# A seventh row block of the gated layer by seven products, with the mixing between its last rounds and a ring of eleven pieces

## The chip, the cores and the metric

The kernel runs on one core of a Trainium2 chip. The metric is the device time of one execution in microseconds (us). TensorE (PE) multiplies, VectorE (DVE) and ScalarE (ACT) do the element-wise work and empty PSUM, GpSimd (POOL) does some element-wise work and issues some DMAs from its own queue, SyncE (SP) issues the rest. Every engine works its own list of instructions strictly in order; they meet only through semaphores.

## The reference

The input x has 8192 rows of 256 numbers. With `xn = layernorm(x)`:

```
feats   = rfs(xn);  weights = rfs(input_weights)        # exp(dot products - norms), 256 features
s       = feats @ weights.T                             # "the mixing"
h = silu(xn @ w1.T * s1) * (xn @ w2.T * s2)             # "the gated layer", 256 -> 1024, w1 and w2 ternary
h = gelu(h @ h1.T * s3);  h = gelu(h @ h2.T * s4)       # two square layers 1024 -> 1024, ternary
g = silu(h @ w3.T * s5)                                 # 1024 -> 256
out = x + s * g
```

Everything is float32. The ternary weights are exact in a short format, so the kernel splits each activation in a high part (fp32r) and a low part (fp16) and multiplies both by the same weights: every product below stands for two passes, "high" and "low".

## The kernel before, in words

The rows are worked in 16 halves of 512 rows; two halves (h0, h1) make a tile, so there are eight tiles, t = 0 to 7. A tile runs through four stages on TensorE, one straight after the other:

1. The gated layer. Its 1024 outputs are eight row blocks of 128 (m or p = 0 to 7), each for both halves. In tile 0 each block and half is a "step" (`gate_step`): two products over 256 inputs, in two PSUM banks, 8 matmuls of 128 x 512. In tiles 1 to 7 the first SEVEN blocks are worked by a seven-product scheme (`gate_seven`) that takes the 2 x 2 of (w1 and w2) by (both halves) at once: 7 products, high and low, so 14 matmuls for what two steps do in 16. The products of blocks 0 to 3 are in eight rounds (`ROUNDS`), those of the blocks from Q = 4 on in `MORE`, one round for each of the seven products. The remaining blocks (`EIGHT = KH - SEVEN`) are steps. `TURNS` is the hand-written order of steps and later rounds on TensorE. SEVEN is 6 before, so blocks 6 and 7 are four steps in each tile.
2. The mixing (`mix`): for each half 8 products of 128 x 256 in plain float32, 16 matmul records, in two PSUM banks.
3. The two square layers, L = 0 and 1, each by seven products w = 0 to 6 of 512 x 512 (`product`), 32 matmuls of 128 x 512 each. Their weights come piece by piece (256 KB, four pieces k = 0 to 3 for one product) into `ring`, RING = 12 pieces deep.
4. The last layer (`down`), with the seven dot products of the next tile's features between.

A block that is worked by seven products costs the others more than a step does. Four results of 128 x 512 have to be made from two banks: ScalarE copies the first of three of them out of PSUM (`gate_seven` of ScalarE, lines 1132 to 1148; for odd p VectorE copies one of them, line 1601), VectorE adds the second bank (lines 1608, 1611, 1615), ScalarE applies silu to two of them (`gate_silus`, lines 1158 and 1161), and VectorE multiplies (`gate_block`, lines 1622 and 1625). The two steps of a block (one for each half) have two silus from PSUM (line 1129) and two multiplications from PSUM (line 1593) in all.

What follows on VectorE in each tile, in this order: `low` (line 1637) makes the low part of a block pair after ScalarE's `high` (line 1188); `subtract` (line 1662) makes t1 to t4 of the square layer out of the blocks; the sums of the products (line 1670 and on). Product w = 0 takes b11 (blocks 0 to 3 of h0), w = 1 takes b21 (blocks 4 to 7 of h0), w = 2 takes t2 = b22 - t1 and w = 3 takes t1 = b12 - b11. TensorE waits at the start of a product for both of its high parts, and before its first low pass, 8 matmuls in, for both of its low parts.

The ring. Piece n may be loaded once piece n - RING has been used for the last time, which is near the end of its product, since the last block of columns needs all four pieces. SP loads the pieces that lie in HBM as sums (`feed`, line 488). In tile 0 the raw pieces (products 0, 1 and 6 of the first layer, 0 and 1 of the second) are loaded from the POOL queue instead (`feed_raw`, line 626), and the same queue makes the sums of the weight blocks: `fold_round` (lines 607 to 617) is four additions of 128 x 512 and the store of one k of them, for the two layers rounds 0 to 7. The order on POOL in tile 0 is written out:

```
            for n in range(RAW, NW * Q):        # raw pieces up to 27
                feed_raw(n)
            fold_round(6)
            for n in range(NW * Q, NW * Q + Q): # 28 to 31
                feed_raw(n)
            fold_round(7)
```

Then come the raw pieces 32 to 35 (second layer, product 1), the load of w3 and its casts (lines 742 and 747), and the rows of the next tile on their way through HBM (`rows_out`, `rows_in`, lines 634 and 643), for which VectorE waits in `turn_blocks` (line 1578). Pieces 36 to 39 are the second layer's product 2.

POOL also finishes the previous tile's output: `gate_y` (line 650) and `add_y` (line 656), each four operations of 128 x 256, for one half after the other. The second pair starts when ScalarE has done `silu_out` (line 1224) in the gated stage. The buffer that they read is later t1.

Of the kernel before, what the change touches and what calls it, by code (L numbers as in the profile page):

```python
# [10 lines left out]
NB = T // P  # L11
KD = D // P
KH = H // P
Q = KH // 2
# [16 lines left out]
RING = 12  # L31
# [29 lines left out]
SEVEN = 6  # L61
EIGHT = KH - SEVEN
FIRST_BANK, OTHER_BANK = (7, 5, 2, 3, 0, 1), (4, 6, 0, 1, 2, 3)
# [10 lines left out]
TURNS = [("step", 0), ("round", 0), ("round", 1), ("step", 1), ("round", 2), ("round", 3), ("step", 2), ("round", 4), ("step", 3),  # L74
         ("round", 5), ("round", 6)]


GATED = {(m, j): i for i, (m, j) in enumerate([(0, 0), (0, 1), (1, 0), (1, 1), (6, 0), (2, 0), (2, 1), (7, 0), (3, 0), (3, 1),
                                               (6, 1), (7, 1), (4, 0), (4, 1), (5, 0), (5, 1)])}
# [3 lines left out]
PAIRS = [(4, 6), (7, 5), (4, 6), (7, 5)]  # L83
# [29 lines left out]
def build(nc, x, win, proj, cols_in, w3s_in, wT, out):  # L113
# [4 lines left out]
    with ExitStack() as ctx:  # L118
# [120 lines left out]
        def seven_places(t, p):  # L239

            b11, b12, b21, b22, t2 = (quad[at[t][0][n]] for n in ("b11", "b12", "b21", "b22", "t2"))
            if p < Q:
                return b11[:, p, :], b12[:, p, :], b22[:, p, :], t2[:, p, :]
            return b21[:, p - Q, :], b22[:, p - Q, :], t2[:, p - 2, :], t2[:, p - Q, :]
# [80 lines left out]

        def n_step(t, n):

            return n + 1 if t == 0 else 2 * KH + 2 * EIGHT * (t - 1) + n + 1
# [5 lines left out]
        def n_third(t, p):  # L334

            return SEVEN // 2 * (t - 1) + p // 2 + 1

# [468 lines left out]
        def _(e):  # L806
# [60 lines left out]
            def gate_seven(t, turn, lows):  # L867
# [6 lines left out]
                for p, n, g, begun in [(p, n, (lows, 1 - lows)[g], g) for g in range(2) for p, n in turn]:  # L874
                    cols_p = slice(p * P, (p + 1) * P)
                    done = n_seven(t, p)
                    bank = OTHER_BANK[p] if n in (1, 3, 6) else FIRST_BANK[p]
                    if begun:
                        pass
                    elif n < 2 and p < Q:  # L880
                        first_free(t, bank)
                    elif n < 2:
                        on.wait_ge((g_c12, g_silu0)[n], n_seven(t, p - 2))
                    elif n == 2:
                        on.wait_ge(t_lo, 2 * t)
# [27 lines left out]
            def mix(t, h, banks):  # L913
# [17 lines left out]
            def bank_free(t, L, w, m):  # L931

                if w == 0 and L == 0:
                    if t == 0:
                        on.wait_ge(*((turned_f, 4) if m < 2 else ((silu, gated)[m - 2], 2 * KH - 1)))
                    else:
                        on.wait_ge((g_silu0, g_c12)[m // 2], n_seven(t, Q + m % 2))
                elif w == 0:
                    on.wait_ge(gelu["b21"], n_block(t, 0, m))
                elif w == 1 and L == 0:  # L940
                    on.wait_ge(mixed, 4 * t + m + 1)
# [108 lines left out]
            for t in range(NT):  # L1050
# [34 lines left out]
                mix(t, h0, (4, 5))  # L1085
                mix(t, h1, (6, 7))
# [29 lines left out]
        def _(e):  # L1116
# [14 lines left out]
            def gate_seven(t, turn):  # L1131

                for p, n in turn:
# [11 lines left out]
                    elif n == 4 and p % 2 == 0:  # L1145
                        if p >= Q:
# [3 lines left out]
            def gate_silus(t, part, ps_):  # L1150

                for p in ps_:
                    _, _, c21, c22 = seven_places(t, p)
                    if part == 0:
                        on.wait_ge(strassen_mm, n_turn(t, p, 5))
                        if p >= Q:
# [14 lines left out]
            def high(t, L, w, g):  # L1171
# [4 lines left out]
                elif L == 0:  # L1176
                    on.wait_ge(gated, n_gate(2 * t + int(name[2]) - 1, Q * (int(name[1]) - 1) + 2 * g + 1))
# [116 lines left out]
            for t in range(NT):  # L1294
# [20 lines left out]
                if t:  # L1315
# [20 lines left out]
                for n in range(0 if t else KH):  # L1336
# [15 lines left out]
                mixed_out(t, h0, (4, 5))  # L1352
                if t:
                    high(t, 0, 1, 0)
                mixed_out(t, h1, (6, 7))
# [99 lines left out]
        def _(e):  # L1455
# [130 lines left out]
            def gate(t, n):  # L1586
# [3 lines left out]
                on.wait_ge(silu, n_step(t, n))  # L1590
                if t == 0 and name == "b22":
# [25 lines left out]
            def gate_block(t, p):  # L1617

                c11, c12, c21, c22 = seven_places(t, p)
                on.wait_ge(g_silu0, n_seven(t, p))  # L1620
                on.wait_ge(g_c11, n_seven(t, p))
                e.scalar_tensor_tensor(out=c11, in0=c11, scalar=scale_col(1, p), in1=c21, op0=ALU.mult, op1=ALU.mult).then_inc(gated, 1)
                on.wait_ge(g_silu1, n_seven(t, p))
                on.wait_ge(g_c12, n_seven(t, p))
                e.scalar_tensor_tensor(out=c12, in0=c12, scalar=scale_col(1, p), in1=c22, op0=ALU.mult, op1=ALU.mult).then_inc(gated, 1)
# [20 lines left out]
            def subtract(t, L, i, g):  # L1646

                for name in SUMS[i][1:]:
                    if name[0] == "t":
                        on.wait_ge(block_sum, n_sum(t, L, int(name[1]) - 1, g))  # L1650
                    elif L == 0:
                        on.wait_ge(gated, n_gate(2 * t + int(name[2]) - 1, Q * (int(name[1]) - 1) + 2 * g + 1))
# [4 lines left out]
                elif L == 0 and i == 0:  # L1657
                    on.wait_ge(pool_out, NB * (n_y(2 * t - 2) + 1))
                if t == 0 and L == 0 and i == 1:
# [118 lines left out]
            for t in range(NT):  # L1778
# [33 lines left out]
                if t:  # L1812
# [199 lines left out]
```

## Time and profile before

| | us |
|---|---|
| median of 3 runs | 1257.03 (1256.8 to 1257.27) |
| the profiled execution's own time | 1258.56 |
| its span | 1256.8 |
| TensorE busy in the span | 1245.0 (99%) |
| VectorE busy | 1023.1 (81%) |
| ScalarE busy | 925.2 (74%) |
| GpSimd busy | 277.1 (22%) |

The span is the stretch from the first to the last instruction of the profiled execution; its own time is what was measured for that same execution. Busy time is the union of an engine's instructions. The mean granted TensorE clock was 0.999 of full speed (2.4 GHz).

### The profile page before, as it was taken

The page shows a single profiled execution, that of the slowest core. Times are in us where ns is not written, and L with a number is a line of the kernel's source. Part 1 is how long each engine was busy: PE and PEld are TensorE (multiplying, and loading weights), DVE is VectorE, ACT ScalarE, POOL GpSimd, SP SyncE. Part 2 cuts the span into 40 slices and gives each one's busy share as a digit, 9 for nine tenths or more (in the row PEclk, how much of TensorE's full clock was granted, in tenths as well). Part 3 has the DMA queues.
Part 4 walks back from the last instruction along what each step waited for, and adds up shares of the span by engine and source line. Part 5 has one row for each costly group of instructions (what it writes and reads, how often), then busy time and mean ns, then how long its engine had stood idle before and what let it go on. Part 6 is the DMA issues. An engine that isn't in the chain of part 4 may idle for free.

```text
span 1256.8 us, 16576 instructions
## 1 busy us (share of the span) xinstructions
PE 1245.0 (99%) x5982; PEld 821.0 (65%) x5982; DVE 1023.1 (81%) x1406; ACT 925.2 (74%) x1405; POOL 277.1 (22%) x325
## 2 busy tenths in 40 slices
PE   8999999999999999999999999999999999999997
PEld 6665676666766666666666666666676666766666
DVE  7979879877898778977889778888788877887675
ACT  4556667788677796777877778777787777787664
POOL 7964322020221102211022110311104030040000
PEclk9999999999999999999999999999999999999999
DMA  9589942575225752257413574145731466323431
GB/s 353 222 334 287 330 171 84 174 228 167 110 96 167 221 184 79 101 187 228 164 68 128 182 231 138 68 143 185 233 118 68 165 189 216 109 84 135 148 137 36
DMA packets 97351, 209.48 MB, mean 167 GB/s; under 512 B 13424, under 2 KB 16624, under 8 KB 96240
## 3 DMA queue, kind: packets, MB, share of 16 engines
q1 hardware_dynamic: 80032, 156.98, 36.7%
q0 software_dynamic: 17232, 51.39, 13.4%
q8 instruction: 49, 0.80, 0.2%
q14 instruction: 38, 0.31, 0.1%
HBM read 175.78 MB, written 38.83 MB: 171 GB/s over the span
## 4 chain that ended last, share of the span: by engine, by line
PE 96%; DVE 2%; DMA 1%; ACT 1%; issue 0%; SPq 0%
PE ps L971 62%; PE ps L899 11%; PE ps L1030 9%; PE ps L827 6%; PE ps L926 4%; DMA quad<-in_win 1%; PE ps L1006 0%; PE ps L1003 0%; PE ps L995 0%; PE ps L992 0%; PE ps L987 0%; PE ps L984 0%; PE ps L999 0%; DVE split_lo L1637 0%; DMA xin<-in_x 0%
## 5 line engine op out<-in xcount | busy, mean ns | idle before, releaser
L971 PE MATMUL ps<-split_hi,ring 128*128 128x512 f32 x1792 | 453.5, 404 | 1.4 <-ACT split_hi L1188 1.4
L971 PE MATMUL ps<-split_lo,ring 128*128 128x512 f16 x1792 | 406.3, 380 | 0.0
L971 PEld LDWEIGHTS ps<-split_hi,ring 128*128 128x128 f32 x1792 | 336.8, 188 | 83.8 <-ACT split_hi L1188 1.9
L1637 DVE SCALAR_TENSOR_TENSOR split_lo<-quad,split_hi 128x1024 f16<-128x1024 f32 x224 | 278.9, 1253 | 131.0 <-ACT split_hi L1188 130.4
L971 PEld LDWEIGHTS ps<-split_lo,ring 128*128 128x128 bf16 x1792 | 166.5, 98 | 214.2 <-issue 29.4
L1188 ACT ACTIVATE split_hi<-quad 128x1024 fp32r<-128x1024 f32 x224 | 231.6, 1048 | 33.7 <-PE ps L971 32.0
L1232 ACT ACTIVATE quad<-quad,cols_s 128x512 f32<-128x512 f32 x192 | 136.3, 719 | 51.8 <-DVE quad L1670 29.5
L1662 DVE TENSOR_TENSOR quad<-quad 128x1024 f32<-128x1024 f32 x128 | 157.2, 1261 | 0.0
L650 POOL TENSOR_TENSOR quad<-quad,s 128x256 f32<-128x256 f32 x56 | 52.0, 957 | 382.6 <-ACT quad L1224 382.6
L634 POOL DMA_DIRECT2D z_h<-xin x56 | 55.7, 1001 | 99.6 <-DVE xin L1498 99.6
L684 POOL DMA_DIRECT2D seen<-in_h x32 | 17.6, 551 | 250.0 <-ACT signs L1269 250.0
L1240 ACT ACTIVATE quad<-ps 128x512 f32<-128x512 f32 x64 | 38.3, 598 | 43.4 <-PE ps L971 43.4
L1244 ACT ACTIVATE quad<-ps 128x512 f32<-128x512 f32 x64 | 38.0, 593 | 30.4 <-PE ps L971 29.9
L926 PE MATMUL ps<-WS,quad 128*128 128x256 f32 x256 | 56.7, 379 | 0.4 <-ACT quad L1351 0.4
L926 PEld LDWEIGHTS ps<-WS,quad 128*128 128x128 f32 x256 | 48.6, 190 | 8.4 <-ACT quad L1351 1.2
L1643 DVE SCALAR_TENSOR_TENSOR split_lo<-quad,split_hi 128x1024 f16<-128x1024 f32 x34 | 40.8, 1221 | 16.3 <-ACT split_hi L1203 16.3
L1673 DVE TENSOR_TENSOR quad<-ps,quad 128x512 f32<-128x512 f32 x64 | 43.9, 686 | 12.4 <-ACT quad L1244 11.8
L827 PE MATMUL ps<-xT_hi,w 128*128 128x512 f32 x176 | 50.0, 411 | 0.8 <-ACT xT_hi L1291 0.8
L1242 ACT ACTIVATE quad<-ps 128x512 f32<-128x512 f32 x64 | 38.0, 594 | 16.1 <-PE ps L971 15.8
L1030 PE MATMUL ps<-w,split_hi 128*128 128x256 f32 x272 | 49.5, 325 | 0.0
L1246 ACT ACTIVATE quad<-ps,cols_s 128x512 f32<-128x512 f32 x64 | 42.6, 680 | 8.4 <-PE ps L971 8.4
L656 POOL TENSOR_TENSOR res<-res,quad 128x256 f32<-128x256 f32 x56 | 46.1, 856 | 1.1
(206 smaller groups left out, 1821.5 us busy)
## 6 DMA issues: line engine op xcount, KB each, us to landing
ring<-hs SPq DMA_DIRECT2D x428, 256.0 KB, 3.7
xin<-in_x SPq DMA_DIRECT2D x16, 512.0 KB, 4.1
s_h<-s SPq DMA_DIRECT2D x16, 512.0 KB, 2.6
seen<-in_h POOLq DMA_DIRECT2D x32, 256.0 KB, 3.9
res<-in_x SPq DMA_DIRECT2D x15, 512.0 KB, 5.5
out<-res SPq DMA_DIRECT2D x15, 512.0 KB, 3.1
z_h<-xin POOLq DMA_DIRECT2D x56, 128.0 KB, 4.0
xT_hi<-z_h POOLq DMA_DIRECT2D x14, 512.0 KB, 6.3
```

The source lines that it names most:

```text
L634: e.dma_start(z_h[j][:, :, :, c, :].rearrange("a i n j -> i n a j"), xin[j][32 * c:32 * c + 32, :, :].rearrange("i b (k a j) -> i (b k) a ...
L650: e.tensor_tensor(y_of(h)[:, b, :], y_of(h)[:, b, :], s[h % 2][:, b, :], ALU.mult).then_inc(pool_y, 1)
L656: e.tensor_tensor(res[:, b, :], res[:, b, :], y_of(h)[:, b, :], ALU.add).then_inc(pool_out, 1)
L827: mm = e.matmul(ps[:, bank, :], weights, moving, start=first and k == 0, stop=last and k == KD - 1, skip_group_check=h == 0 and m == 0)
L899: mm = e.matmul(ps[:, bank, :], short(weights) if g else weights, moving, start=n in (0, 1, 3) and not begun, stop=n in (1, 5, 6) and begu ...
L926: mm = e.matmul(ps[:, banks[b // 2], (b % 2) * D:(b % 2 + 1) * D], quad[at[t][0]["v"]][:, KD * j + r, b * P:(b + 1) * P], WS[:, r, :], sta ...
L971: mm = e.matmul(ps[:, 4 * (w % 2) + m, :], weights, moving, start=first and k == 0 and begins, stop=last and k == Q - 1 and not begins, sk ...
L1030: mm = e.matmul(ps[:, bank, col:col + D], part[:, k, tokens], moving[:, Q * kq + k, :], start=not last and col == 0 and k == 0 and g == 0, ...
L1188: e.activation(both(slots_hi[i], g), both(quad[at[t][L][name]], g), ACT.Identity, scale=POWER[L]).then_inc(hi, 1)
L1232: e.activation(q[:, m, :], q[:, m, :], ACT.Gelu, scale=col).then_inc(gelu[name], 1)
L1637: e.scalar_tensor_tensor(out=both(slots_lo[i], g), in0=both(quad[at[t][L][FAST[w][1]]], g), scalar=POWER[L], in1=both(slots_hi[i], g).bitc ...
L1662: e.tensor_tensor(dst, a, b, ALU.subtract).then_inc(block_sum, 1)
```

## The change

SEVEN goes from 6 to 7: in tiles 1 to 7 block 6 is worked by seven products too, and one step for each half (block 7) remains. `wsum`, the sums of the gate weights, grows from 768 to 896 columns in each of three rows, and RING goes from 12 to 11. In the new `TURNS` the mixing of h0 comes between rounds 4 and 5 of `MORE` and that of h1 after round 6, and other PSUM banks are used. ScalarE's `silu_out` moves behind its second step, and its and VectorE's orders are rewritten; VectorE does the second halves of the blocks 4 to 6 (needed for h1) after the low parts of b21. Block 6 uses two of the rows of t1's buffer for its silus, and waits for `pool_out` there. Tile 0 has the same steps, rounds and mixing as before.

```diff
-RING = 12
+RING = 11
-SEVEN = 6
+SEVEN = 7
 EIGHT = KH - SEVEN
-FIRST_BANK, OTHER_BANK = (7, 5, 2, 3, 0, 1), (4, 6, 0, 1, 2, 3)
+FIRST_BANK, OTHER_BANK = (7, 5, 2, 3, 7, 0, 1), (4, 6, 0, 1, 5, 2, 3)
-TURNS = [("step", 0), ("round", 0), ("round", 1), ("step", 1), ("round", 2), ("round", 3), ("step", 2), ("round", 4), ("step", 3),
-         ("round", 5), ("round", 6)]
+TURNS = [("step", 0), ("round", 0), ("round", 1), ("round", 2), ("step", 1), ("round", 3), ("round", 4), ("mix", 0), ("round", 5),
+         ("round", 6), ("mix", 1)]
-PAIRS = [(4, 6), (7, 5), (4, 6), (7, 5)]
+PAIRS = [(4, 6), (4, 6)]
+MIX0, MIX = ((4, 5), (6, 7)), ((4, 6), (7, 5))
@@ seven_places
             if p < Q:
                 return b11[:, p, :], b12[:, p, :], b22[:, p, :], t2[:, p, :]
+            if p == SEVEN - 1:
+                t1 = quad[at[t][0]["t1"]]
+                return b21[:, p - Q, :], b22[:, p - Q, :], t1[:, 3, :], t1[:, 2, :]
             return b21[:, p - Q, :], b22[:, p - Q, :], t2[:, p - 2, :], t2[:, p - Q, :]
@@ TensorE, gate_seven
+                    elif n < 2 and p == Q:
+                        on.wait_ge(g_silu0, n_seven(t, n))
                     elif n < 2:
-                        on.wait_ge((g_c12, g_silu0)[n], n_seven(t, p - 2))
+                        on.wait_ge((g_c12, g_silu0)[n], n_seven(t, p - 3))
@@ TensorE, mix
-                        elif b // 2 == j:
-                            on.wait_ge(silu, n_step(t, 2 + j))
+                        elif j == 0:
+                            on.wait_ge(*((silu, n_step(t, 1)), (gated, n_gate(*step_of(t, 1))))[b // 2])
                         else:
-                            on.wait_ge(gated, n_gate(*step_of(t, 3 - j)))
+                            on.wait_ge((g_silu0, g_c12)[b // 2], n_seven(t, Q))
@@ TensorE, the turns
+                    elif kind == "round":
+                        gate_seven(t, MORE[n], i % 2)
                     else:
-                        gate_seven(t, MORE[n], i % 2)
+                        mix(t, 2 * t + n, MIX[n])
@@ ScalarE
                     gate_seven(t, MORE[0])
+                    gate_silus(t, 1, (2, 3))
+                    gate_seven(t, MORE[2])
+                    gate_silu(t, 1)
                     silu_out(h0 - 2)
-                    gate_silus(t, 1, (2, 3))
-                    gate_silu(t, 1)
-                    gate_seven(t, MORE[2])
-                    gate_silu(t, 2)
                     gate_seven(t, MORE[4])
                     high(t, 0, 0, 0)
-                    gate_silu(t, 3)
-                    gate_silus(t, 0, (4, 5))
-                    gate_silus(t, 1, (4, 5))
                     high(t, 0, 0, 1)
+                    gate_silus(t, 1, (4,))
+                    gate_silus(t, 0, (4, 5, 6))
+                    gate_silus(t, 1, (5, 6))
@@ VectorE
                     gate_block(t, 1)
+                    gate(t, 0)
                     gate_seven(t, MORE[1])
-                    gate(t, 0)
                     gate_block(t, 2)
+                    gate_block(t, 3)
                     gate(t, 1)
-                    gate_block(t, 3)
                     gate_seven(t, MORE[4])
-                    gate(t, 2)
                     low(t, 0, 0, 0)
-                    gate(t, 3)
+                    low(t, 0, 0, 1)
                     gate_seven(t, MORE[6])
-                    gate_block(t, 4)
-                    gate_block(t, 5)
-                    low(t, 0, 0, 1)
+                    for p in range(Q, SEVEN):
+                        gate_block(t, p, (0,))
                     low(t, 0, 1, 0)
                     low(t, 0, 1, 1)
+                    for p in range(Q, SEVEN):
+                        gate_block(t, p, (1,))
```

## Rows read from the trace of the kernel before

**Rows 1.** The page's busy times: us, share of the span, instructions.

```profile
PE 1245.0 (99%) x5982; PEld 821.0 (65%) x5982; DVE 1023.1 (81%) x1406; ACT 925.2 (74%) x1405; POOL 277.1 (22%) x325
```

**Rows 2.** The page's chain that ended last, shares by engine.

```profile
PE 96%; DVE 2%; DMA 1%; ACT 1%; issue 0%; SPq 0%
```

**Rows 3.** Stretch, length, busy PE, PEld, DVE, ACT, POOL (instructions), clock, DMA share, GB/s.

```profile
487.01:499.63 12.62, 12.62 (x59) 7.79 (x57) 8.78 (x15) 10.23 (x17) 5.78 (x8) 1.00 0.40 159
499.63:513.15 13.52, 13.52 (x62) 8.11 (x61) 13.52 (x20) 11.53 (x20) 8.48 (x10) 1.00 0.01 4
513.15:519.87 6.72, 6.72 (x34) 5.92 (x32) 6.72 (x10) 5.12 (x8) 0.07 (x1) 1.00 0.64 226
519.87:541.29 21.42, 21.42 (x98) 13.49 (x97) 17.77 (x23) 16.08 (x25) 0.54 (x1) 1.00 0.38 136
```

**Rows 4.** PE in order of time, tile 3: start, us, line, operation, [idle before].

```profile
536.17 3.63 PE L971 MATMUL ps<-split_lo,ring 128*128 128x512 f16 x16
```

**Rows 5.** VectorE in order of time, tile 3, same columns.

```profile
502.25 0.74 DVE L1622 SCALAR_TENSOR_TENSOR quad<-quad,cols_s 128x512 f32<-128x512 f32 x1
...
508.97 1.22 DVE L1625 SCALAR_TENSOR_TENSOR quad<-quad,cols_s 128x512 f32<-128x512 f32 x1
...
514.36 1.27 DVE L1615 TENSOR_TENSOR quad<-ps,quad 128x512 f32<-128x512 f32 x2
...
521.83 1.22 DVE L1637 SCALAR_TENSOR_TENSOR split_lo<-quad,split_hi 128x1024 f16<-128x1024 f32 x1 [1.28 <-ACT split_hi L1188]
522.98 6.89 DVE L1662 TENSOR_TENSOR quad<-quad 128x1024 f32<-128x1024 f32 x6
...
532.18 1.21 DVE L1637 SCALAR_TENSOR_TENSOR split_lo<-quad,split_hi 128x1024 f16<-128x1024 f32 x1
```

**Rows 6.** ScalarE in order of time, tile 3.

```profile
503.42 1.10 ACT L1224 ACTIVATE quad<-quad 128x1024 f32<-128x1024 f32 x1
...
520.25 0.60 ACT L1214 ACTIVATE s<-ps 128x512 f32<-128x512 f32 x1 [1.06 <-PE ps L926]
...
538.36 1.05 ACT L1188 ACTIVATE split_hi<-quad 128x1024 fp32r<-128x1024 f32 x1
```

**Rows 7.** POOL in order of time, tile 3.

```profile
504.59 3.72 POOL L650 TENSOR_TENSOR quad<-quad,s 128x256 f32<-128x256 f32 x4 [11.73 <-ACT quad L1224]
508.39 3.78 POOL L656 TENSOR_TENSOR res<-res,quad 128x256 f32<-128x256 f32 x4
```

**Rows 8.** POOL in order of time, tile 0.

```profile
85.63 2.12 POOL L626 DMA_DIRECT2D ring<-in_h  x4
...
105.05 2.13 POOL L626 DMA_DIRECT2D ring<-in_h  x4
107.13 0.94 POOL L742 DMA_DIRECT2D w<-in_w  x1
```

**Rows 9.** PE in order of time, tile 0.

```profile
83.83 4.02 PE L971 MATMUL ps<-split_hi,ring 128*128 128x512 f32 x16
...
108.89 2.11 PE L971 MATMUL ps<-split_hi,ring 128*128 128x512 f32 x8 [1.44 <-ACT split_hi L1188]
...
114.12 4.03 PE L971 MATMUL ps<-split_hi,ring 128*128 128x512 f32 x16
```

**Rows 10.** Ring loads from POOL's queue, 104 to 108.5 us: issue to landing.

```profile
DMA to landing us min/median/max: 5.3/7.2/9.8
```

**Rows 11.** Ring loads from SP's queue, 115 to 118 us.

```profile
DMA to landing us min/median/max: 9.1/9.3/9.6
```

**Rows 12.** Ring load from SP's queue issued at 64.0 us.

```profile
DMA to landing us min/median/max: 8.4/8.4/8.4
```

**Rows 13.** Ring loads from SP's queue, 180 to 1250 us.

```profile
DMA to landing us min/median/max: 2.7/3.6/7.3
```

**Rows 14.** VectorE in order of time, tile 0, turning the next rows.

```profile
143.81 1.29 DVE L1578 STREAM_TRANSPOSE xin<-xT_hi 128x512 f32<-128x512 f32 x2
```

**Rows 15.** VectorE's low parts (L1637): durations in ns, min/median/max.

```profile
L1637 DVE SCALAR_TENSOR_TENSOR split_lo<-quad,split_hi x224: 1204/1224/2983, 29.9 to 1225.7; 128x1024 f16<-128x1024 f32 x112
```

More of the change, by code:

```diff
@@ L72 @@
 TURN = {pn: i for i, pn in enumerate(sum(ROUNDS + MORE, []))}
-TURNS = [("step", 0), ("round", 0), ("round", 1), ("step", 1), ("round", 2), ("round", 3), ("step", 2), ("round", 4), ("step", 3),
-         ("round", 5), ("round", 6)]
-GATED = {(m, j): i for i, (m, j) in enumerate([(0, 0), (0, 1), (1, 0), (1, 1), (6, 0), (2, 0), (2, 1), (7, 0), (3, 0), (3, 1),
-                                               (6, 1), (7, 1), (4, 0), (4, 1), (5, 0), (5, 1)])}
+TURNS = [("step", 0), ("round", 0), ("round", 1), ("round", 2), ("step", 1), ("round", 3), ("round", 4), ("mix", 0), ("round", 5),
+         ("round", 6), ("mix", 1)]
+GATED = {(m, j): i for i, (m, j) in enumerate([(0, 0), (0, 1), (1, 0), (1, 1), (7, 0), (2, 0), (2, 1), (3, 0), (3, 1), (7, 1),
+                                               (4, 0), (5, 0), (6, 0), (4, 1), (5, 1), (6, 1)])}
 PAIRS0 = [((6, 7), (4, 5), (2, 3))[n % 3] for n in range(2 * KH)]
-PAIRS = [(4, 6), (7, 5), (4, 6), (7, 5)]
+PAIRS = [(4, 6), (4, 6)]
+MIX0, MIX = ((4, 5), (6, 7)), ((4, 6), (7, 5))
 class Once:
@@ L324, in n_gate, with n_gate_both @@
             return 2 * KH * t + GATED[m, j] + 1
+        def n_gate_both(h, m):
+            return max(n_gate(h, m), n_gate(h, m + 1))
         def n_step(t, n):
@@ L334, in n_third @@
         def n_third(t, p):
-            return SEVEN // 2 * (t - 1) + p // 2 + 1
+            return (SEVEN + 1 - p % 2) // 2 * (t - 1) + p // 2 + 1
         def n_turn(t, p, n):
@@ L936, in bank_free @@
                     else:
-                        on.wait_ge((g_silu0, g_c12)[m // 2], n_seven(t, Q + m % 2))
+                        on.wait_ge((g_silu0, g_c12)[m // 2], n_seven(t, Q + 1 + m % 2))
                 elif w == 0:
@@ L940, in bank_free @@
                 elif w == 1 and L == 0:
-                    on.wait_ge(mixed, 4 * t + m + 1)
+                    on.wait_ge(mixed, 4 * t + ((0, 3, 1, 2)[m] if t else m) + 1)
                 elif w == 1:
@@ L1084, in _ @@
                     dots(h1, (6, 7))
-                mix(t, h0, (4, 5))
-                mix(t, h1, (6, 7))
+                    mix(t, h0, MIX0[0])
+                    mix(t, h1, MIX0[1])
                 for L in range(2):
@@ L1145, in gate_seven @@
                     elif n == 4 and p % 2 == 0:
-                        if p >= Q:
+                        if p == SEVEN - 1:
+                            on.wait_ge(pool_out, NB * (n_y(2 * t - 1) + 1))
+                        elif p >= Q:
                             on.wait_ge(gated, n_gate(2 * t + 1, p - Q))
@@ L1155, in gate_silus @@
                         on.wait_ge(strassen_mm, n_turn(t, p, 5))
-                        if p >= Q:
+                        if p == SEVEN - 1:
+                            on.wait_ge(pool_out, NB * (n_y(2 * t - 1) + 1))
+                        elif p >= Q:
                             on.wait_ge(gated, n_gate(2 * t + 1, p - 2))
@@ L1176, in high @@
                 elif L == 0:
-                    on.wait_ge(gated, n_gate(2 * t + int(name[2]) - 1, Q * (int(name[1]) - 1) + 2 * g + 1))
+                    on.wait_ge(gated, n_gate_both(2 * t + int(name[2]) - 1, Q * (int(name[1]) - 1) + 2 * g))
                 else:
@@ L1351, in _ @@
                         e.activation(quad[at[0][0]["v"]][:, n, :], stage[n % 2][:, :], ACT.Exp).then_inc(feat, 1)
-                mixed_out(t, h0, (4, 5))
+                mixed_out(t, h0, (MIX if t else MIX0)[0])
                 if t:
                     high(t, 0, 1, 0)
-                mixed_out(t, h1, (6, 7))
+                mixed_out(t, h1, (MIX if t else MIX0)[1])
                 if t:
@@ L1590, in gate @@
                 on.wait_ge(silu, n_step(t, n))
+                if t and name == "b22":
+                    on.wait_ge(gated, n_gate(2 * t, m - Q))
                 if t == 0 and name == "b22":
@@ L1615, in gate_seven, with gate_block @@
                         e.tensor_tensor(c12, B, c12, ALU.add).then_inc(g_c12, 1)
-            def gate_block(t, p):
+            def gate_block(t, p, halves=(0, 1)):
                 c11, c12, c21, c22 = seven_places(t, p)
[L1620 to L1625, printed above, removed]
+                if 0 in halves:
+                    on.wait_ge(g_silu0, n_seven(t, p))
+                    on.wait_ge(g_c11, n_seven(t, p))
+                    e.scalar_tensor_tensor(out=c11, in0=c11, scalar=scale_col(1, p), in1=c21, op0=ALU.mult, op1=ALU.mult).then_inc(gated, 1)
+                if 1 in halves:
+                    on.wait_ge(g_silu1, n_seven(t, p))
+                    on.wait_ge(g_c12, n_seven(t, p))
+                    e.scalar_tensor_tensor(out=c12, in0=c12, scalar=scale_col(1, p), in1=c22, op0=ALU.mult, op1=ALU.mult).then_inc(gated, 1)
             def rows_sums_low(t):
@@ L1651, in subtract @@
                     elif L == 0:
-                        on.wait_ge(gated, n_gate(2 * t + int(name[2]) - 1, Q * (int(name[1]) - 1) + 2 * g + 1))
+                        on.wait_ge(gated, n_gate_both(2 * t + int(name[2]) - 1, Q * (int(name[1]) - 1) + 2 * g))
                     else:
@@ L1658, in subtract @@
                     on.wait_ge(pool_out, NB * (n_y(2 * t - 2) + 1))
+                    on.wait_ge(gated, n_gate(2 * t + 1, SEVEN - 1))
                 if t == 0 and L == 0 and i == 1:
```

## The prediction
> **What bounds the kernel now.** I read the page's busy times first: TensorE 99% of the span, VectorE 81%, ScalarE 74% [rows 1]. The chain of waits agrees: 96% of it is TensorE [rows 2]. So time can be saved only by fewer matmuls, and is lost whenever TensorE waits for something that it does not wait for now. The second reading is by stretch, in tile 3, whose pattern all tiles 1 to 7 repeat [rows 3]: the eight rounds of blocks 0 to 3 (487.01 to 499.63), the turns (to 513.15), the mixing (to 519.87), three products (to 541.29). TensorE is busy in all of it, but in the turns VectorE is busy 13.52 of 13.52 us and ScalarE 11.53. VectorE enters the square layers with a debt that it pays off by the third product: there it still has 17.77 of 21.42. That debt decides what the change is worth in a tile.
>
> **What is removed from TensorE.** In each of seven tiles two steps of 8 matmuls go and 14 matmuls of one more block come: 2 fewer, and 9 changes between high and low in the turns instead of 11. The rounds have 56 matmuls in 12.62 us, the turns 28 + 32 = 60 in 13.52 us [rows 3]: 0.225 us each in both, so 2 are 0.45 us. From below: at the mixing's rate, 6.72/32 = 0.21 us, a matmul costs that much bare, the turns' other 0.92 us would be their 11 changes at 0.08, and two matmuls with two changes are 0.59 us. I take 0.5 us a tile, 3.5 us in all (3.2 to 4.1). The mixing's 32 records stay and only move.
>
> **What is added in tiles 1 to 7.** ScalarE gets 5 operations for block 6 (three copies, two silus) and loses 2 silus; VectorE gets 5 and loses 2. On VectorE that is 3 x 0.6 to 0.66 us, about 1.9 us a tile, in a stretch where it has no gap. What was cover is also cut: before, all 6.72 us of mixing lay between the last round and product 0; after, only one half's 3.36 us. Against that, 4 multiplications of the gate blocks were slowed by POOL: such a one takes 0.74 us, and 1.22 us beside POOL's output work [rows 5, 7]; after the change `silu_out` stands behind the second step, which ends 34 matmuls into the turns (499.63 + 34 x 0.225 = 507.3), and its silu of 0.6 us: 507.9 instead of 503.42 [rows 6], and POOL starts 4.5 us later, when all but the last of these blocks are done.
>
> I lay out VectorE's new order in tile 3's clock, with durations less some 0.08 us where instructions follow each other (6 subtractions in 6.89 us are 1.15 each; adds 0.60, gate blocks 0.66, low parts 1.14) [rows 5]. Round 6 now ends at 519.87 - 0.5 - 3.36 = 516.0. The three sums of round 6 run from about 515.8 to 517.6 (before, two, from 514.36 [rows 5]), the three first-half blocks to 519.6. `low` of b21's first pair follows its high part, to 521.2. The second waits: ScalarE takes it after the two evictions of h1's mixing, of which the last waits for TensorE, as it did before (520.25 [rows 6]); its high part ends at 522.0, the low part at 523.1, against 523.05 before. Then come three second-half blocks (2.0), six subtractions (6.9), two statistics (0.66), low part of t2, a sum (0.60), second low part of t2: 535.6. Before, that one ended at 532.18 + 1.21 = 533.4 [rows 5], so VectorE is 2.2 us later. TensorE's first low pass of product 2 came at 536.17 [rows 4] and now would at 535.65. The cover of 2.8 us is gone: wait 0 to 0.2. Product 3 is next: its high parts stand on ScalarE behind gelus that wait for VectorE's sums, so they move about 2 us with them, from 538.36 + 1.05 = 539.4 [rows 6] to 541.3 or 541.4; product 3 began at 541.29 [rows 3] and now would at 540.8. Wait 0.5 us. From product 4 on VectorE has caught up. The POOL window now covers the low parts of b11; such a part takes 1.2 us free and up to 2.98 beside POOL [rows 15]. There is 1.3 us of idle before round 6's sums to hide it, so I add nothing, 0.4 us at the most. So a tile waits 0.5 us more (bounds 0 and 1.2), seven 3.5 us (0 to 8.4). The gain of the fewer matmuls and this wait cancel.
>
> The Trainium skill (SBUF, Who interferes with whom) says that a VectorE instruction with two SBUF inputs contends with a GpSimd one that reads SBUF, and that one of them blocks for the whole of the other. By it each of the two low parts could stand behind a whole POOL operation, an estimate of 0.93 us each from POOL's own rows, 0.6 us more than the idle hides in a tile. The row of 1.22 instead of 0.74 us shows less than a whole operation; the sum above goes by the rows.
>
> **What the ring of eleven does.** In tiles 1 to 7 the last piece of product w + 2 is now ordered at the end of product w instead of a product earlier. A product is 21.42/3 = 7.14 us [rows 3], so it has 7.14 + 0.6 + 0.6 us to land. These loads take 3.6 us, at most 7.3 [rows 13]: hidden, nothing.
>
> Tile 0 is another matter, though it has no seven-product block. Three places:
>
> First, piece 11. It was loaded with the first twelve; now it waits for product 0's end, 64.0 us. A load issued just then took 8.4 us [rows 12], so it lands at 72.4. Product 2 starts at 57.10 + 2 x 7.14 = 71.4 (products follow from 83.83, in whose sixteen matmuls product 3 ends at 85.66 [rows 9]) and wants it at 72.0. Cost 0.4 us (0 to 1).
>
> Second, POOL's queue. `feed_raw(27)` stands before `fold_round(6)`. It waited for piece 15, used up at the end of product 3, and was the fourth of the loads from 85.63, at 87.2 [rows 8]. With eleven it waits for piece 16, used up at the end of product 4: 92.3. Everything behind it on POOL moves by 5.1 us: round 6, raw pieces 28 to 31, round 7, raw pieces 32 to 35, the load of w3, the next rows. Pieces 28 to 31 go out from 100.9 to 102.5 and are wanted from 108.9 to 109.5 [rows 9]; with the landings of rows 10 up to their median they are at most 0.2 us late. Pieces 32 to 35 went out from 105.05 and now would from 110.2 to 111.8; they landed in 5.3 to 9.8 us [rows 8, 10]. The second layer's product 1 starts at 108.89 + 7.14 = 116.0 [rows 9] and wants its fourth piece 0.65 us in. At the shortest landing, piece 35 is there at 117.1, wait 0.4; at the longest at 121.6, wait 4.9. As SP's loads of that time also take 9.1 to 9.6 us [rows 11], I take 3.5 us. A second way leads to the same size: the rows of tile 1 pass the same queue, VectorE takes them up at 143.81 without waiting [rows 14], and 5.1 us later they would hold it up in front of sums for which TensorE waits.
>
> Third, piece 39, ordered at the end of the second layer's product 0 and behind the store of round 7; it takes 9.3 us [rows 11], to 125 or, with the store late, 128 us. Product 2 would want it at 123.8, or 127.3 after the wait above. 0.4 us more (0 to 1.2).
>
> The wider `wsum` makes four POOL additions in tile 0 a sixth longer, some 1.4 us together, before the DMA store and the ring for which POOL waits anyway: nothing. Tile 0's sum is 0.4 + 3.5 + 0.4 = 4.3 us (0.4 to 7.1).
>
> **The sum.** 4.3 - 3.5 + 3.5 = +4.3 us, and 0.2 us for what of POOL's window is not hidden. The profiled execution took 1258.56 us, 1.76 over its span; the median is 1257.03, 1.5 us under it. A difference of 4.5 us does not depend on which one I start from: 1263.1 for the profiled one, 1261.5 us for the median.
>
> **The rivals.**
> *TensorE's count decides, and all else stays hidden.* For it: 99% busy, and idle of 1.28 us before one low part [rows 5] that can be filled. Against it: piece 35 late even at the shortest landing. 1257.0 - 3.5 + 0.4 = about 1253.8. Chance 0.12.
> *The steady tiles gain in full, tile 0 pays.* If VectorE's 2.2 us are 1.5, the waits of products 2 and 3 vanish: 1257.0 - 3.5 + 4.3 = 1257.8. Chance 0.20.
> *VectorE's debt is larger in every tile.* At product 3's start TensorE waits for t1's high part. It decides once the debt is over 2 us; each us more costs 7. With 1 us more than I count (the low parts beside POOL, a late piece of round 6): 1261.5 + 7 = 1268.5. Chance 0.15.
> *A long wait in tile 0 costs twice.* If the granted clock falls to its lower level (half of 2.4 GHz) after the 3.5 us, the matmuls behind it take twice as long; half a product so worked adds 3.6 us: 1265. The one wait of 1.44 us [rows 9] left the clock at 1.00, and no row here is at the lower level. Chance 0.08.
> The Trainium skill (TensorE: Matmul & The Clock Gate, Why this matters for your kernels) advises against idle gaps of TensorE between its bursts of matmuls, since the clock falls after them; that is this last rival, and no row here shows it.
>
> **How the numbers follow.** The forecast has 0.45, the rivals 0.12, 0.20, 0.15 and 0.08. A measurement of this kernel can tell 0.2%, 2.5 us, from no change. Faster than 1254.5: the first rival and a little of the second, 0.15. Within: most of the second, and the forecast's lower edge, 0.23. Slower: 0.62. Range: 1254.5, where a tile waits nothing and tile 0 pays 1 us, to 1267, where tiles wait 0.9 us and tile 0 pays 6.5. The forecast's own is 1259.5 to 1264.
>
> **What would show it.** Right: TensorE idle in tile 0 at product 1 of the second layer, released by DMA; POOL's round 6 starting near 92.8; turns plus mixing 0.5 us shorter in each tile; TensorE idle of a few tenths before products 2 or 3, released by ScalarE's split or VectorE's. Wrong: no idle in tile 0 beyond the 1.44 us, or products 2 and 3 following without a gap.

## The result and the profile after

The changed kernel takes 1263.43 us (median of 5 runs, 1262.64 to 1265.88) against 1257.09 us; the ratio is 1.005, with a 95% interval of 1.0039 to 1.0062. It is 6.3 us slower; the forecast was 4.5 us slower. The profiled execution is the slowest of the five: 1265.88 us, with a span of 1264.1 us. Its busy times, from the page's first part:

```profile
PE 1247.3 (99%) x5968; PEld 820.4 (65%) x5968; DVE 1034.6 (82%) x1427; ACT 932.4 (74%) x1426; POOL 278.7 (22%) x325
```

Against [rows 1] TensorE has 14 matmuls fewer (5968 for 5982), as counted, and is busy 2.3 us more. The profiled spans differ by 7.3 us. By stretches, from the starts of the products, of the tiles' rounds and of the last layer's last stretch (1238.84 us before, 1245.81 after):

| Stretch, us | before | after | difference |
|---|---|---|---|
| start to product 0 of tile 0 | 57.10 | 57.78 | +0.7 |
| from there to tile 1's rounds | 122.81 | 128.66 | +5.85 |
| tiles 1 to 6, each | 153.67 | 153.81 | +0.15, six times +0.9 |
| tile 7, to its last layer | 136.92 | 136.49 | -0.4 |
| the rest of the last layer | 17.92 | 18.27 | +0.35 |

The first line is chance: in the eight experiments below, with either kernel's code up to there, product 0 starts between 55.3 and 56.9 us, so both profiles here start it late. Nearly all of the loss is in tile 0, where the diff changes only the ring and the width of `wsum`.

**Tiles 1 to 7.** The stretches that answer to [rows 3], in tile 3, which starts 6.80 us later (columns as there). The mixing of h0 now lies in the second of them and that of h1 in the third, so the two are to be taken together:

```profile
493.81:506.41 12.60, 12.60 (x59) 7.79 (x57) 8.76 (x15) 10.22 (x17) 5.76 (x8) 1.00 0.44 158
506.41:519.80 13.39, 13.39 (x61) 8.93 (x60) 12.81 (x21) 12.06 (x21) 3.87 (x6) 1.00 0.00 0
519.80:526.22 6.42, 6.42 (x31) 4.89 (x31) 5.96 (x8) 4.68 (x9) 4.77 (x5) 1.00 0.29 87
526.22:547.90 21.68, 21.63 (x98) 13.47 (x96) 18.88 (x23) 15.44 (x24) 0.54 (x1) 1.00 0.54 181
```

From the first round to product 0 are 32.41 us instead of 32.86: 0.45 us gained. In the three products (the last line) VectorE is busy 18.88 us instead of 17.77: that is the debt, work that it has still to do when the square layers begin. Its instructions in order of time (start, us, line, operation, [idle before]):

```profile
519.19 3.04 DVE L1657 SCALAR_TENSOR_TENSOR split_lo<-quad,split_hi 128x1024 f16<-128x1024 f32 x2
...
522.69 1.89 DVE L1633 TENSOR_TENSOR quad<-ps,quad 128x512 f32<-128x512 f32 x3 [0.47 <-PE ps L910]
...
532.27 6.90 DVE L1683 TENSOR_TENSOR quad<-quad 128x1024 f32<-128x1024 f32 x6
...
541.47 1.21 DVE L1657 SCALAR_TENSOR_TENSOR split_lo<-quad,split_hi 128x1024 f16<-128x1024 f32 x1
```

ScalarE's high part of t1, for which product 3 waits:

```profile
547.22 1.05 ACT L1205 ACTIVATE split_hi<-quad 128x1024 fp32r<-128x1024 f32 x1
```

And the waits of TensorE's weight loads from 526 to 549 us (who, for whom: us in all, times, longest):

```profile
PEld ps L982 <- DVE split_lo L1657: 0.7, 2, 0.5
PEld ps L982 <- ACT split_hi L1205: 0.5, 1, 0.5
```

Put back by these 6.80 us, the second low part of t2 ends at 542.68 - 6.80 = 535.9 us (forecast 535.6; it was 533.4), and t1's high part at 548.27 - 6.80 = 541.5 (forecast 541.3 to 541.4). The waits are those of the side that loads weights; the matmuls themselves start some 0.2 us late in product 2 and 0.4 us late in product 3. So a tile gains 0.45 us and loses 0.6. The two low parts of b11 beside POOL took 3.04 us instead of some 2.4, mostly out of VectorE's idle time, of which 0.47 us were left.

**Tile 0.** POOL in order of time:

```profile
86.53 1.59 POOL L635 DMA_DIRECT2D ring<-in_h  x3 [0.84 <-PE ps L982]
93.44 0.54 POOL L635 DMA_DIRECT2D ring<-in_h  x1 [5.32 <-PE ps L982]
93.99 1.32 POOL L616 TENSOR_TENSOR early<-early 128x512 f32<-128x512 f32 x1
...
109.56 2.14 POOL L635 DMA_DIRECT2D ring<-in_h  x4
```

Of the four loads that stood together in [rows 8], the fourth, piece 27, now waits 5.32 us for a matmul, and the additions of round 6 behind it start at 93.99. Pieces 32 to 35 go out from 109.56 instead of 105.05: the additions took less time than before, so that of 6.2 us at round 6 (93.99 for 87.75) 4.5 are left, and 3.8 reckoned from product 0. The chain of waits has the last of them (start, us, engine, operation):

```profile
111.12 11.88 DMA ring<-in_h
```

and TensorE in the second layer's products 0 and 1 answers to [rows 9]:

```profile
111.81 2.85 PE L982 MATMUL ps<-split_hi,ring 128*128 128x512 f32 x8 [3.69 <-ACT split_hi L1205]
114.46 4.57 PE L982 MATMUL ps<-split_lo,ring 128*128 128x512 f16 x16
118.67 2.21 PE L982 MATMUL ps<-split_hi,ring 128*128 128x512 f32 x8
121.25 0.70 PE L982 MATMUL ps<-split_hi,ring 128*128 128x512 f32 x2 [0.36 <-DMA ring<-in_h]
123.04 1.66 PE L982 MATMUL ps<-split_hi,ring 128*128 128x512 f32 x6 [1.09 <-DMA ring<-in_h]
```

Piece 35 was ordered at 111.12 and landed at 123.0 us. Without a wait TensorE would have taken it up where before did, 116.0 + 0.65 + 0.7 (the later start) = 117.3 us. That is 5.7 us, nearly the whole loss of tile 0. Two things stand in front of it and cost nothing more. One is a wait of 3.69 us for the high part of the second layer's first product, where [rows 9] has 1.44. The other is the clock behind that wait, the third number from the end of these rows (stretches of 1 us, columns as in [rows 3]):

```profile
113.00:114.00 1.00, 1.00 (x4) 0.73 (x3) 1.00 (x2) 1.00 (x2) 0.00 (x0) 0.50 1.23 358
...
115.00:116.00 1.00, 1.00 (x4) 0.36 (x3) 1.00 (x2) 0.00 (x0) 0.00 (x0) 0.50 0.96 317
116.00:117.00 1.00, 1.00 (x5) 0.43 (x4) 0.41 (x1) 0.58 (x2) 0.00 (x0) 0.82 1.09 317
```

It was granted at 0.50, the lower of the two levels (1.2 of 2.4 GHz), for some 3.4 us. TensorE came later to the piece that was not there yet, and waited less for it.

### The profile page after: what moved, and what is told of

It is laid out like the page before. It is cut to its first block, busy times and chain, and to the rows that moved or that the text cites. A ratio compares the mean times of both kernels' runs of the same rounds, so it can differ in the third digit from the quotient of the medians.

```text
span 1264.1 us, 16605 instructions
## 1 busy us (share of the span) xinstructions
PE 1247.3 (99%) x5968; PEld 820.4 (65%) x5968; DVE 1034.6 (82%) x1427; ACT 932.4 (74%) x1426; POOL 278.7 (22%) x325
## 4 chain that ended last, share of the span: by engine, by line
PE 92%; ACT 2%; DMA 2%; DVE 2%; POOL 1%; issue 1%; SPq 0%
PE ps L982 58%; PE ps L910 12%; PE ps L1041 9%; PE ps L937 4%; PE ps L836 4%; DMA ring<-in_h 1%; ACT quad L1249 1%; DMA quad<-in_win 1%; DVE quad L1691 1%; DVE split_lo L1657 1%; PE ps L1014 0%; PE ps L998 0%; ACT split_hi L1205 0%; PE ps L1003 0%; PE ps L1017 0%
## 5 line engine op out<-in xcount | busy, mean ns | idle before, releaser
L659 POOL TENSOR_TENSOR quad<-quad,s 128x256 f32<-128x256 f32 x56 | 45.5, 842 | 416.6 <-ACT quad L1241 416.6
L1257 ACT ACTIVATE quad<-ps 128x512 f32<-128x512 f32 x64 | 38.3, 598 | 39.7 <-PE ps L982 39.7
L1261 ACT ACTIVATE quad<-ps 128x512 f32<-128x512 f32 x64 | 38.0, 594 | 30.5 <-PE ps L982 29.9
L665 POOL TENSOR_TENSOR res<-res,quad 128x256 f32<-128x256 f32 x56 | 53.1, 979 | 1.1
L1694 DVE TENSOR_TENSOR quad<-ps,quad 128x512 f32<-128x512 f32 x64 | 43.8, 685 | 7.6 <-ACT quad L1261 7.0
L1041 PEld LDWEIGHTS ps<-w,split_hi 128*128 128x128 f32 x272 | 36.8, 190 | 13.8 <-issue 13.7
L1691 DVE TENSOR_TENSOR quad<-ps,quad 128x512 f32<-128x512 f32 x64 | 42.4, 681 | 2.8 <-PE ps L982 2.8
## 6 DMA issues: line engine op xcount, KB each, us to landing
z_h<-xin POOLq DMA_DIRECT2D x56, 128.0 KB, 4.1
```

The source lines that it names most:

```text
L665: e.tensor_tensor(res[:, b, :], res[:, b, :], y_of(h)[:, b, :], ALU.add).then_inc(pool_out, 1)
L1041: mm = e.matmul(ps[:, bank, col:col + D], part[:, k, tokens], moving[:, Q * kq + k, :], start=not last and col == 0 and k == 0 and g == 0, ...
L1691: e.tensor_tensor(quad[v][:, m, :], here, quad[v][:, m, :], ALU.add).then_inc(c_sum["b11"], 1)
```

## The experiments

The kernel before ran beside all of them: median 1257.63 us beside the first four (27 runs, 1256.57 to 1259.5), 1257.52 us beside the last four (18 runs, 1256.61 to 1258.69). The changed kernel was not run again beside them; before stood 0.4 to 0.5 us higher there than in the first comparison, and differences to the changed kernel are uncertain by about as much. Tile 0 is from product 0 to tile 1's rounds, the period is that of tiles 1 to 6, both from the one profiled execution of each. That execution lies 2.4 us above the median for the changed kernel and for "mixes last", 1.5 to 1.6 above it for before and "both of these", and within 0.4 us of it for the other experiments.

| Kernel | median us | ratio (95%) | tile 0 | period |
|---|---|---|---|---|
| before | 1257.09 | | 122.8 | 153.67 |
| changed | 1263.43 | 1.005 (1.0039 to 1.0062) | 128.7 | 153.81 |
| ring of eleven alone | 1262.96 | 1.0045 (1.0031 to 1.0059) | 128.0 | 153.66 |
| changed, POOL's order | 1259.06 | 1.001 (1.0001 to 1.0019) | 125.0 | 153.79 |
| changed, t3 later | 1259.78 | 1.0019 (1.001 to 1.0028) | 128.4 | 153.20 |
| changed, both of these | 1256.18 | 0.9992 (0.9983 to 1.0001) | 125.3 | 153.19 |
| changed, statistics later | 1266.54 | 1.008 (1.0066 to 1.0093) | 130.5 | 153.81 |
| changed, mixes last | 1265.27 | 1.006 (1.0046 to 1.0074) | 130.5 | 154.05 |
| before, t3 later | 1257.37 | 1.0 (0.9991 to 1.0009) | 122.8 | 153.67 |
| all that helps together | 1254.08 | 0.9974 (0.9963 to 0.9984) | 123.3 | 153.20 |

### The ring of eleven alone

```
-RING = 12        (in the kernel before)
+RING = 11
```

> The kernel before with a ring of eleven pieces and nothing else. Theory (tile 0 pays for the ring, the seventh block pays and costs about nothing in tiles 1 to 7): POOL's fold round 6 moves from 87.8 to about 93, the second layer's pieces 32 to 35 land near 121 to 123, TensorE waits in tile 0 for 4 to 6 us more; time 1257.1 + 5 = 1261 to 1263; tiles 1 to 7 as before, period 153.66 us. Rival (the ring is hidden, the loss comes from the seventh block): 1257 to 1258.

One constant costs 5.3 of the 6.3 us (1262.96 - 1257.63). Tile 0 is 5.2 us longer and the period the same to 0.01 us. TensorE, same columns as above:

```profile
109.58 3.26 PE L971 MATMUL ps<-split_hi,ring 128*128 128x512 f32 x8 [3.69 <-ACT split_hi L1188]
...
120.14 1.66 PE L971 MATMUL ps<-split_hi,ring 128*128 128x512 f32 x6 [0.82 <-DMA ring<-in_h]
```

The same two waits stand in the same places, for a high part and for a piece. At least 5.2 us of tile 0's loss are the ring's, and in tiles 1 to 6 the ring costs nothing.

### The late loads taken out of the way of POOL's additions

In the changed kernel piece 27 is ordered ahead of all of fold round 6, and piece 31 ahead of round 7, so the round stands behind the piece's wait. Here each is taken out of its loop and ordered inside the round, ahead of the fourth addition (`load_round` was never called there, `beside` was None):

```
-                    load_round(beside)
+                    feed_raw(beside)
...
-            for n in range(RAW, NW * Q):
+            for n in range(RAW, NW * Q - 1):
...
-            fold_round(6)
-            for n in range(NW * Q, NW * Q + Q):
+            fold_round(6, NW * Q - 1)
+            for n in range(NW * Q, NW * Q + Q - 1):
...
-            fold_round(7)
+            fold_round(7, NW * Q + Q - 1)
```

> The changed kernel with POOL's order in tile 0 rewritten: piece 27 is loaded inside fold round 6 and piece 31 inside fold round 7 (ahead of the fourth addition), so that neither round stands behind its wait. Theory: POOL is only 1 to 2 us later than in the kernel before, pieces 32 to 35 land by 118, tile 0 loses 0 to 2 us instead of 5 to 6; time 1257.1 + 0.2 x 6 - 0.4 + 1 = 1258 to 1259.5. Rival (fewer pieces ahead are late by themselves, or the DMA queues are full): 1262 to 1264.

It took 4.4 us less than the changed kernel, tile 0 is 3.7 us shorter, and the period is unchanged. So most of the cost is not that there are fewer pieces as such, but that the wait for one holds up the rest of the queue. POOL in order of time:

```profile
84.27 1.60 POOL L635 DMA_DIRECT2D ring<-in_h  x3 [1.55 <-PE ps L982]
85.85 1.32 POOL L616 TENSOR_TENSOR early<-early 128x512 f32<-128x512 f32 x1
...
104.27 2.19 POOL L635 DMA_DIRECT2D ring<-in_h  x4
```

The additions follow the third load at once, and pieces 32 to 35 go out at 104.27. TensorE no longer waits for a DMA in front of product 1. What is left of the loss, 2.2 us, is 0.6 us more of the wait for the high part (2.07 us for 1.44) and a lower clock behind it, from 108.4 to 111.9 us, which costs half of that time (TensorE, and the stretch from 109 to 112 us):

```profile
107.92 3.38 PE L982 MATMUL ps<-split_hi,ring 128*128 128x512 f32 x8 [2.07 <-ACT split_hi L1205]
...
109.00:112.00 3.00, 3.00 (x9) 1.70 (x8) 3.00 (x4) 1.55 (x3) 0.00 (x0) 0.53 1.04 294
```

### t3's sum moved a product later

```
-                                elif w == 0:
-                                    subtract(t, 0, 2, m - 2)
+                                elif w == 0 and t == 0:
+                                    subtract(t, 0, 2, m - 2)
+                                elif t and w == 1 and m >= 2:
+                                    subtract(t, 0, 2, m - 2)
```

> The changed kernel with the two subtractions for t3 on VectorE moved in tiles 1 to 7 from product 0 to product 1, behind the low parts of t2. Theory (VectorE's debt makes TensorE wait 0.2 us in product 2 and 0.4 us before product 3): both waits go, 0.6 us a tile in six tiles, 3.6 us; time 1263.4 - 3.6 = 1259.8. Rival (the wait before product 3 hangs on ScalarE's own order): 1263.

The period fell from 153.81 to 153.20 us: 0.61 us a tile, the two waits above. It took 3.65 us less than the changed kernel. Against before the period is 0.47 us shorter, so that is what the seventh block is worth in a tile once nothing waits. Tile 0 has the same code as in the changed kernel; this profile, near the median, shows 128.4 us for it where that of the changed kernel's slowest execution shows 128.7.

### Both

> Both of the last two edits on the changed kernel. Theory: they are in different tiles and add up; 1257.1 + 1 - 0.44 x 7 = about 1255, under both kernels. Rival: the waits only move, 1258 to 1260.

The two single gains are 4.4 + 3.7 = 8.1 us. Together they are 7.3, and the time lies 1.2 us over the forecast. The kernel is 1.4 us under before in its medians, but the interval just reaches 1. Tile 0 is still 2.5 us too long:

```profile
109.26 2.14 PE L982 MATMUL ps<-split_hi,ring 128*128 128x512 f32 x8 [2.06 <-ACT split_hi L1205]
...
118.39 1.66 PE L982 MATMUL ps<-split_hi,ring 128*128 128x512 f32 x6 [1.20 <-DMA ring<-in_h]
```

The wait for the high part is as long as with POOL's order alone (2.06 for 2.07 us), but the clock stayed at 1.00 here: the 8 matmuls behind it took 2.14 us and not 3.38. Instead TensorE meets a wait of 1.20 us for the last piece, which took 11.1 us to land and not 9.6.

### The row statistics of tile 0 later

Why does that high part come late? VectorE and POOL of the changed kernel at that time:

```profile
102.45 2.12 DVE L1540 SCALAR_TENSOR_TENSOR sm<-sm 128x8 f32<-128x8 f32 x1
...
104.81 1.12 DVE L1544 SCALAR_TENSOR_TENSOR sm<-sm 128x8 f32<-128x8 f32 x1
...
106.45 0.85 DVE L1540 SCALAR_TENSOR_TENSOR sm<-sm 128x8 f32<-128x8 f32 x1
...
107.54 1.14 DVE L1544 SCALAR_TENSOR_TENSOR sm<-sm 128x8 f32<-128x8 f32 x1
...
103.23 1.31 POOL L616 TENSOR_TENSOR early<-early 128x512 f32<-128x512 f32 x1
104.62 1.28 POOL L618 TENSOR_TENSOR early<-early 128x512 f32<-128x512 f32 x1
```

The same in the kernel before:

```profile
100.82 0.66 DVE L1524 SCALAR_TENSOR_TENSOR sm<-sm 128x8 f32<-128x8 f32 x1
...
101.72 1.13 DVE L1528 SCALAR_TENSOR_TENSOR sm<-sm 128x8 f32<-128x8 f32 x1
...
103.08 1.12 DVE L1526 TENSOR_TENSOR sm<-sm 128x8 f32<-128x8 f32 x1
```

These are VectorE instructions on 8 numbers a partition; the median of their lines is 0.17 us. Four took 0.85 to 2.12 us here, 4.5 us too much in all; before, three took 0.66 to 1.13, 2.4 us too much. The difference, 2.1 us, is nearly what the wait for the high part grew by (1.44 to 3.69). The first two shown end at 104.57 and 105.93 us, POOL's two additions at 104.54 and 105.90. The Trainium skill (SBUF, Who interferes with whom) says that a VectorE instruction with two SBUF inputs and a GpSimd one that reads SBUF exclude each other for a whole instruction. The trace agrees with these two ends; but the one of 2.12 us began 0.8 us before POOL's addition, while POOL still ordered DMAs. The statistics stand in front of the sum from which the late high part is made. So they were moved behind it:

```
-... (0, 5, 2): (6, 7), (0, 5, 3): (8, 9),
-             (1, 0, 2): (10,), (1, 0, 3): (11,), (1, 1, 2): (12,), (1, 1, 3): (13,)}
+... (1, 0, 2): (6, 7), (1, 0, 3): (8, 9),
+             (1, 1, 2): (10, 11), (1, 1, 3): (12, 13)}
```

> The changed kernel with six of the small statistics operations of tile 0 moved on VectorE from the first layer's product 5 to the second layer's products 0 and 1. Theory (tile 0's end is set by pieces 32 to 35 landing near 121 to 123; the wait of 3.7 us before the second layer and the lower clock after it lie in front of that and cost nothing of their own): that wait shrinks to under 1 us, the wait for the DMA grows to 4 or 5 us, time 1262 to 1263.5, as the changed kernel. Rival (the waits add up): 3 to 4 us less, 1259.5.

It took 3.1 us more than the changed kernel, 1.8 of them in tile 0 by the profiles, and both theories missed. The wait in front of product 0 shrank to 0.35 us, now for a piece, but three of POOL's four additions of round 7 took 2.15 us each now, and pieces 32 to 35 went out from 110.80, with product 0 starting 1.3 us earlier. TensorE, and the clock behind its wait:

```profile
112.39 2.20 PE L982 MATMUL ps<-split_hi,ring 128*128 128x512 f32 x8
...
119.87 4.19 PE L982 MATMUL ps<-split_hi,ring 128*128 128x512 f32 x8 [5.28 <-DMA ring<-in_h]
...
119.80:126.00 6.20, 6.07 (x13) 3.11 (x14) 0.17 (x1) 0.00 (x0) 0.00 (x0) 0.50 1.31 377
```

The wait of 5.28 us for the DMA is nearly all that is left of waiting. The 6.2 us behind it at clock 0.50 do the work of some 3 us, and nothing is waited for after them: this lower level costs in full. It outweighs that the last piece, though ordered 2.5 us later reckoned from product 0, landed 0.6 us earlier (it took 8.7 us and not 11.9). The Trainium skill (TensorE: Matmul & The Clock Gate, Why this matters for your kernels) advises against idle gaps of TensorE between bursts of matmuls because the clock falls after them; these rows agree.

### The mixes after the last round

`TURNS` ends on `("round", 4), ("round", 5), ("round", 6), ("mix", 0), ("mix", 1)`; all else is the changed kernel's.

> The changed kernel with both halves' mixing after round 6, as in the kernel before. Theory (the low part of b21's second pair waits for the evictions of the mixing wherever it stands, so VectorE's debt is the same): waits of 0.6 us a tile stay, period 153.8, time as the changed kernel, within 1 us. Rival (the cover of 3.36 us more lets VectorE start the last sums earlier): 0.6 us a tile less, 1259.8.

It took 1.8 us more than the changed kernel, and the period is 0.24 us longer, which is 1.4 us in six tiles. Both theories missed. The waits in the square layers went, but now rounds 5 and 6 follow round 4 at once and wait for their banks (TensorE's waits from 494 to 548 us):

```profile
PEld ps L910 <- ACT quad L1163: 0.7, 1, 0.7
...
PEld ps L910 <- DVE quad L1629: 0.4, 1, 0.4
...
PE ps L910 <- ACT quad L1163: 0.3, 1, 0.3
```

From a tile's first round to its product 0 it is 33.2 us instead of 32.4. So the mixing between the rounds was cover for the work that empties their banks. Tile 0, where nothing was changed, took 130.5 us in this profile, that of the slowest execution. There the clock was at 0.50 a second time, from 121.8 to 125.2 us, behind waits of 0.62 and 1.10 us for pieces, as it was not in the changed kernel's profile behind 0.36 and 1.09; half of these 3.4 us is nearly all by which tile 0 is longer than in the changed kernel.

### t3's sum moved in the kernel before

> The kernel before with t3's subtractions moved as in e3. Theory (before, no wait of TensorE hangs on VectorE in tiles 1 to 7): no change, 1257 to 1257.6, period 153.66. Rival (VectorE's order hides some loss there too): 2 us less.

No change: ratio 1.0, period 153.67 us in both. The order of the sums is worth something only with the debt that the seventh block brings.

### All that helps, together

The edits of the fourth and the fifth experiment, and fold round 7 orders pieces 31 to 34 inside it, where the fourth has piece 31 alone; only piece 35 stays behind the round:

```
-                if beside is not None:
-                    load_round(beside)
+                for n in beside or ():
+                    feed_raw(n)
...
+            fold_round(6, (NW * Q - 1,))
...
+            fold_round(7, range(NW * Q + Q - 1, NW * Q + 2 * Q - 1))
...
-                    for n in range(NW * Q + Q, 2 * NW * Q):
+                    for n in range(NW * Q + 2 * Q - 1, 2 * NW * Q):
```

> The changed kernel with both edits of e4, the statistics moved as in e5, and pieces 31 to 34 all loaded inside fold round 7. Theory: pieces 32 to 34 go out 3 us earlier, only piece 35 is left behind, tile 0 loses under 1 us against the kernel before; time 1254 to 1255. Rival (the DMA queues are full then, so that the pieces land no earlier, or piece 39 becomes late): 1256.

1254.08 us (8 runs, 1253.51 to 1255.48): 3.4 us faster than before and 9.3 faster than the changed kernel. Tile 0 is 0.5 us longer than before's, the period 0.47 shorter. POOL and TensorE:

```profile
101.29 2.17 POOL L635 DMA_DIRECT2D ring<-in_h  x4 [0.30 <-POOL early L620]
...
105.65 0.54 POOL L635 DMA_DIRECT2D ring<-in_h  x1
...
115.19 1.64 PE L982 MATMUL ps<-split_hi,ring 128*128 128x512 f32 x6 [1.94 <-DMA ring<-in_h]
```

Reckoned from product 0 of tile 0, which started 2.5 us earlier here, the first of the late loads, piece 32, goes out 5.2 us earlier than in the changed kernel, and the last, piece 35, 3.0; a wait of 1.94 us for that last one is left, behind which the clock stayed at 1.00. A seventh block with a ring of twelve was not tried. The wider `wsum` takes 384 more numbers a partition, and a piece of the ring has 512.

## Why the prediction came out right, step by step

- **Fewer matmuls, 0.5 us a tile.** Measured 0.45 us in the stage, 0.47 us in the period once the waits are gone (the third experiment).
- **VectorE's debt, waits of 0.5 us a tile in seven.** Measured 0.6 us in six, in the places forecast and with times right to 0.3 us; moving work of VectorE behind them took them away, so that they were its debt is shown. Tile 7 has no statistics in its square layers, showed no such wait and gained 0.4 us. The sum over tiles 1 to 7 is +0.5 us, for a forecast of 0 and 0.2 us for POOL's window.
- **POOL's queue, 3.5 us.** The mechanism was right: the wait for piece 27 (5.32 us) holds up the queue, and the first experiment gives that to the ring alone. The shift forecast for all behind it, 5.1 us, was too large for the late loads: reckoned from product 0 they went out 3.8 us later. The mis-sized term is the landing of piece 35, and it outweighs that. It was taken within 5.3 to 9.8 us [rows 10], and was 11.88. The cost was 5.7 us in the profile and 5.2 in the first experiment, above the 4.9 set as its upper end. Why it landed so late is not shown; a copy of 1 MB from SP's queue was ordered half a us ahead of these loads. The second way to this size, through the rows of tile 1, cost nothing of its own: VectorE takes them up without waiting, at 150.34 us, as far behind product 1 as before.
- **Pieces 11 and 39, 0.4 us each.** Neither is waited for. Piece 11 went out at 64.7 and landed in 6.8 us, before 72.7.
- **The ring in tiles 1 to 7, nothing.** Right: the period of the first experiment is that of before.
- **The wider `wsum`, nothing.** Right as far as it shows. The first experiment, without it, has all but 0.7 us of tile 0's loss, and POOL orders pieces 32 to 35 from 51.8 us behind product 0 in both. The 0.7 us are piece 35's landing, 11.2 us there and 11.9 here; in two more kernels with this tile 0 it is 11.6 and 12.2.
- **The rival with the clock.** The clock fell and it was free, since it stood in front of the late pieces. It followed not the wait for a piece but that of 3.69 us for a high part, whose growth from 1.44 us was not foreseen: a delayed fold round falls otherwise on VectorE's small instructions, and slows four of them and not three. That the forecast took no price for the clock came out right by this order of the waits, which it did not foresee: that was luck. Behind the last wait the lower level does cost: some 3 us in the fifth experiment, 1.7 us in the profile of the sixth.

The sum was 1.8 us short. Tiles 1 to 7 and the landing of piece 35 explain 0.3 and 2.2 us, less the 0.8 us that pieces 11 and 39 did not cost. The one profile of the changed kernel is of its slowest run, 2.4 us over the median. The third experiment's, with the same tile 0 and near its median, has tile 0 only 0.2 us shorter but product 0 of tile 0 1.9 us earlier, so the late start is the larger part of it, as far as one profile tells.

## What to carry to other kernels

One buffer fewer in a ring cost nothing where its loads had a queue to themselves, and 5 us where the load that now waits stood in front of other work: look at what is queued behind it, and let it wait behind that. Where a change brings an engine a debt, move what is needed last behind what is waited for first. A wait, or a lowered clock, in front of a longer wait is free; take the last one away first, or count the others again.

## What the runs showed of the hardware

The granted clock was 0.50 after idle times of TensorE of 3.69 us (four kernels: the changed one, the ring alone, t3 later, mixes last) and 5.28 us, once after 2.07 us (POOL's order) and once after 0.62 and 1.10 us with two matmuls between (mixes last). It stayed at 1.00 after 2.06, 1.94 and 1.44 us, and after 0.36 and 1.09 us with two matmuls between.

Four loads of 256 KB from POOL's queue landed in 5.3 to 9.8 us when ordered from 105.05 us on (before), and in 8.3 to 11.9 us when ordered from 109.56, half a us behind a copy of 1 MB from SP's queue. In the fifth experiment, ordered 3.1 us behind such a copy, they took 7.8 to 8.7 us. What sets this is not isolated.

VectorE instructions of 0.17 us in the median took 0.85 to 2.12 us beside POOL's additions of 1.3 us, and in the fifth experiment three of POOL's own took 2.15 us.
